# Attention values in a vision-transformer kernel: two half-array products per head pair instead of one full-array product

## The reference, cut to what matters

```python
q = (x @ Wq).reshape(b, n, H, DH)      # b = 64 images, n = 17 tokens, H = 16 heads, DH = 64
k = (x @ Wk).reshape(b, n, H, DH)
v = (x @ Wv).reshape(b, n, H, DH)
scores = einsum('bihd,bjhd->bhij', q, k) * scale + bias      # ALiBi slope per head
scores = where(causal, scores, -1e30)
attn = softmax(scores)
out = einsum('bhij,bjhd->bihd', attn, v).reshape(b, n, H * DH)
return out @ Wo + bo
```

## Time and profile before

| what | value |
|---|---|
| median of three runs | 633.22 us (632.42 to 634.51) |
| span of the profiled execution | 671.0 us |
| PE busy / weight loads busy | 545.3 / 438.7 us |
| DVE / ACT / POOL busy | 439.3 / 358.8 / 218.8 us |
| mean granted TensorE clock of the profiled execution | 0.908 |
| line 942 (values), PE passes and busy time | 256, 32.1 us |
| line 1381 (its copies), ACT instructions and busy time | 128, 35.6 us |

### The profile page before, as it was taken

One profiled execution on the slowest core, in us unless ns is written; L12 is line 12 of the kernel. 1 busy time (PEld: TensorE's weight loads), 2 busy tenths in 40 slices (PEclk: granted clock), 3 DMA queues, 4 the chain that ended last, 5 costly groups with the idle time before them and its releaser, 6 DMA issues.

```text
span 671.0 us, 9955 instructions
## 1 busy us (share of the span) xinstructions
PE 545.3 (81%) x3242; PEld 438.7 (65%) x3242; DVE 439.3 (65%) x995; ACT 358.8 (53%) x894; POOL 218.8 (33%) x230
## 2 busy tenths in 40 slices
PE   3969760565546999999999999999889789888976
PEld 3737650133236899999998878776556557566675
DVE  4987998999994455555555137575646646654576
ACT  1667624355546677777773464255545645565610
POOL 2010001134226011111112312566656666666400
PEclk9977985668857999999999999999979989998878
DMA  8960000054000000000000020056646657565583
GB/s 279 382 235 0 1 0 0 0 194 133 2 0 1 24 25 25 24 25 25 1 1 1 1 68 9 18 169 180 183 135 197 169 147 212 163 204 166 144 363 104
DMA packets 43894, 67.31 MB, mean 100 GB/s; under 512 B 11022, under 2 KB 27015, under 8 KB 43716
## 3 DMA queue, kind: packets, MB, share of 16 engines
q1 hardware_dynamic: 36868, 64.62, 30.3%
q0 software_dynamic: 6976, 2.07, 1.5%
HBM read 66.81 MB, written 17.20 MB: 125 GB/s over the span
## 4 chain that ended last, share of the span: by engine, by line
PE 56%; DVE 26%; ACT 6%; issue 5%; another core or an unknown queue 3%; DMA 1%; POOL 1%; SPq 0%; ACTq 0%; DVEq 0%
PE ps L1089 9%; PE ps L736 6%; PE ps L734 6%; PE ps L735 6%; PE ps L953 5%; PE ps L911 4%; PE ps L942 4%; PE ps L741 3%; PE ps L1097 2%; PE ps L925 2%; PE ps L1079 2%; DVE region L1731 2%; PE ps L1136 2%; DVE region L1742 1%
## 5 line engine op out<-in xcount | busy, mean ns | idle before, releaser
L1089 PE MATMUL ps<-region 128*128 128x352 f32 x256 | 93.0, 488 | 5.9 <-issue 3.1
L694 POOL DMA_INDIRECT y_rows<-region x60 | 62.2, 1037 | 58.1 <-ACT region L1433 39.1
L1787 DVE TENSOR_TENSOR region<-ps,region 32x136 f32<-32x136 f32 x128 | 38.1, 297 | 60.1 <-PE ps L911 58.6
L685 POOL DMA_INDIRECT region<-x_rows,region x64 | 68.1, 1064 | 20.2 <-issue 17.4
L734 PE MATMUL ps<-nTh,high 128*128 128x272 f32 (+2 forms) x248 | 74.1, 299 | 0.4 <-ACT region L1362 0.4
L735 PE MATMUL ps<-nTl,high 128*128 128x272 f32 (+2 forms) x248 | 71.7, 289 | 0.0
L644 POOL COPY region<-region 32x544 f32<-32x544 f32 x32 | 26.4, 825 | 122.2 <-DVE region L1806 120.7
L1456 ACT ACTIVATE high<-region 88x512 fp32r<-88x512 f32 x64 | 40.3, 630 | 43.2 <-remote 23.1
L1089 PEld LDWEIGHTS ps<-region 128*128 128x128 f32 x256 | 45.7, 199 | 24.5 <-issue 7.3
L1935 DVE SCALAR_TENSOR_TENSOR region<-region,ps 128x176 f32<-128x176 f32 x64 | 25.3, 396 | 53.3 <-ACT region L1446 24.4
L736 PE MATMUL ps<-nTh,pairs_low 128*128 128x272 f32 x192 | 55.4, 289 | 0.0
(11 more groups left out here) (264 smaller groups left out, 1439.3 us busy)
## 6 DMA issues: line engine op xcount, KB each, us to landing
region<-moe_w SPq DMA_DIRECT2D x64, 352.0 KB
region<-moe_w SPq DMA_DIRECT2D x64, 176.0 KB
y_rows<-zrow SPq DMA_DIRECT2D x1, 6528.0 KB, 25.3
region<-y_rows SPq DMA_DIRECT2D x8, 768.0 KB, 10.7
region<-wqkv SPq DMA_DIRECT2D x8, 384.0 KB, 3.0
region<-ffn_w SPq DMA_DIRECT2D x2, 1024.0 KB, 8.3
region<-patches SPq DMA_DIRECT2D x3, 384.0 KB, 8.3
region<-patches SPq DMA_DIRECT2D x1, 1152.0 KB, 10.7
```

Source lines behind the costliest of these rows:

```text
L685: nc.gpsimd.indirect_dma_start(out=xb[m8], out_offset=None, in_=x_rows, in_offset=bass.IndirectOffsetOnAxis(ap=sloti[:, at:at + 1], axis=0 ...
L694: nc.gpsimd.indirect_dma_start(out=y_rows, out_offset=bass.IndirectOffsetOnAxis(ap=sld[m8], axis=0), in_=yb[m], in_offset=None, bounds_che ...
L1089: mm = nc.tensor.matmul(ps[:, 2 + m % 2, 0:2 * EI], xbT[m % 2][:, c, :], w13[m][:, c, :], start=(c == 0), stop=(c == DC - 1))
L1787: last = V.tensor_tensor(sc[r, s0:s0 + 8, 0:T].rearrange("p (a b) t -> p a b t", a=4), ps[r, 4:8, 0:4 * GW].rearrange("p a (b h t) -> p a ...
```

## The change

The values block has four PSUM banks of eight products in place of eight banks of two. Each product takes one head: 64 stationary columns, 68 moving columns, and a result on partitions 0 to 63 (head 0) or 64 to 127 (head 1) of the same bank and the same columns. The two heads alternate. All 4 x 68 = 272 columns of a bank are then useful, in the order of `attnT`, so ACT empties a bank with one copy of 128 x 272. The fills of a pair go from 24 to 20 (HPF = 5), which moves the semaphore counts, and `scores(1)` comes after the second of four banks instead of the fourth of eight.

```diff
-HPF = 6
+HPF = 5
@@ def attention(n, j):   (and the same count in move and before project)
-                first = 0 if isinstance(n, int) and n == 0 else 4 * HPF * n - 8
+                first = 0 if isinstance(n, int) and n == 0 else 4 * HPF * n - 4
...
                     if n == HP:
-                        pe.wait_ge(s_evac, 4 * HPF * n - 8)
-                    both = pbd[1 - j].rearrange("p (h g) w -> p g h w", h=2)
-                    for g in range(8):
-                        if project and g == 4:
+                        pe.wait_ge(s_evac, 4 * HPF * n - 4)
+                    for g in range(4):
+                        if project and g == 2:
                             scores(1)
                         b = fill(g if not project else 16 + g)
-                        for k in range(2):
-                            mm = nc.tensor.matmul(ps[:, b, 2 * k * GW:2 * (k + 1) * GW].rearrange("p (h w) -> p h w", h=2),
-                                                  vp[1 - j][:, 2 * g + k, :], both[:, 2 * g + k, :, :],
-                                                  start=True, stop=True)
+                        for k in range(4):
+                            for hd in range(2):
+                                f = slice(DH * hd, DH * hd + DH)
+                                mm = nc.tensor.matmul(ps[f, b, k * GW:(k + 1) * GW], vp[1 - j][:, 4 * g + k, f],
+                                                      pbd[1 - j][:, GT * hd + 4 * g + k, :], start=True, stop=True)
                         mm.then_inc(s_fill, 1)
@@ def move(n, j):
                 if not (isinstance(n, int) and n == 0):
-                    for g in range(8):
+                    for g in range(4):
                         act.wait_ge(s_fill, first + 1 + g)
-                        for hd in range(2):
-                            f = slice(DH * hd, DH * hd + DH)
-                            cs = slice(2 * g * GW, 2 * (g + 1) * GW)
-                            dst = attnT[f, n - 1, cs] if isinstance(n, int) else \
-                                attnT[f, bass.ds(n - 1, 1), cs].rearrange("p a b -> p (a b)")
-                            ins = nc.scalar.activation(
-                                dst.rearrange("p (k w) -> p k w", k=2),
-                                ps[f, g % 4, 0:4 * GW].rearrange("p (k h w) -> p k h w", k=2, h=2)[:, :, hd, :], ACT.Copy)
-                        ins.then_inc(s_evac, 1)
+                        nc.scalar.activation(attnT[:, n - 1, 4 * g * GW:4 * (g + 1) * GW], ps[:, g, 0:4 * GW],
+                                             ACT.Copy).then_inc(s_evac, 1)
```

More of the change, by code:

```diff
@@ L959, in _ @@
             pe.wait_ge(s_ext, 2 * HP)
-            pe.wait_ge(s_evac, 4 * HPF * HP - 8)
+            pe.wait_ge(s_evac, 4 * HPF * HP - 4)
             for t in range(4):
```

## The result

The changed kernel takes 622.91 us (median of four runs, 620.44 to 625.0) against 633.78 us (632.42 to 634.51) of the kernel before, run beside it: a ratio of 0.984 with a 95% interval of 0.980 to 0.987, 10.9 us less. The profiled execution of the changed kernel has a span of 623.3 us, near its own runs; that of the kernel before had 671.0.

What follows compares the result with a forecast made beforehand. PE was taken to bound blocks 1 to 7; seven blocks -9.5, last values -2.6 and the stall before the output projection -0.5 gave -12.6 us, 633.2 to 620.6 us; range 618.5 to 636.5 us.

Steps and rivals of the forecast that it cites:

- The overlap: Values of a block: both heads' passes run side by side on array halves, 31 ns each, 1.98 us against 3.71; chance 0.53.
- the turns: Values: the array halves take turns, passes one after another at 59 ns, 633.4 to 636.5 us; chance 0.37.
- The first rival: Values: the halves take turns at 59 ns a pass, +1.9 us, 635.1 us, up to 636.5 with 62 ns; chance 0.37.
- The second and third rivals: Values: each change of half drains, 658 us; or one half's loads stop the other's products, 663 us; together chance 0.07.
- The changes of shape: Switches between full-array and narrow products in a block: four at 0.094 us each, 0.38 us added.
- Copies: ACT's value copies: sixteen become four, 3.1 us less on ACT per block, worth nothing in blocks 1 to 7.
- Last values: Values of n = 8, first pass to line 953: 5.43 us becomes 2.81, -2.6 us.
- The stall before the output projection: Last pass of pair 6's values to line 953: 1.41 us becomes 0.87 as ACT finishes sooner, -0.5 us.
- Waits that come closer: In a block, scores(1) stays hidden behind DVE by 0.2 us; key copies counted as nothing, at worst 0.2 us a block.

Runs made afterwards that it cites:

- e9: Changed kernel with head 1's products sent to head 0's partitions, so all passes use one array half; 1.006 of the kernel before, block period 18.92 us.
- e3: Changed kernel with a block's values in one piece behind both halves of the scores, two shape changes fewer; 0.983 of the kernel before, period 16.96 us.
- e1: Changed kernel with head 0's four products of a bank first, then head 1's four, instead of alternating; 0.994 of the kernel before, block period 17.84 us.
- e8: Changed kernel with the heads alternating after every two products instead of every one; 0.984 of the kernel before, block period 17.16 us.
- e2: Changed kernel with ACT emptying each bank by four copies of 64 x 136 instead of one; 0.988 of the kernel before, block period 17.04 us.
- e5: e3 with ACT's rounding of the next weights moved behind the key copies; 651.5 us, 0.980 of the kernel before, block period 16.71 us.
- e6: Changed kernel with scores(1) in two parts, six shape changes a block instead of four; 0.990 of the kernel before, periods 17.60 and 17.66 us.
- e4: Kernel before, with its full-array products and two copies a bank, in the order of e3; 1.005 of the kernel before, block period 18.52 us.
- e7: Changed kernel with each head's 64 value columns as two products of 32, on array quarters; 0.987 of the kernel before, block period 17.01 us.
- the second group: Kernels run on another chip beside the kernel before; the unchanged changed kernel, rerun there, took 656.3 us against 665.1, ratio 0.987.

## Why the prediction was right

**The overlap** was the step on which all hung, and it held: 32 passes in 0.945 us from first to last start, 29.5 ns each, against 31 forecast. It was inferred from the delays at changes of shape, which is a thin reason, so the choice between it and the turns was partly luck; the range, 618.5 to 636.5 us, holds both. e9 is what shows the overlap, with the same passes at twice the time on one half.

**The first rival** was priced at 635.1 us, up to 636.5. e9 is that case built, at 0.6% over before (0.3 to 0.8), some 637 us on the scale of the first chip. Its kind and sign were right; it was short by the changes of shape. One reason given for it, that PE starts products in order, is what the starts of e1 and e8 speak against. The second and third rivals would have put 0.15 and 0.11 us between starts; the steady ones are 6 or 7 and 53 ns.

**The changes of shape** are the term that was mis-sized: 0.094 us forecast, 0.38 a block. What the rows of before gave me was only the later start of the next product. The second pass after a change is late as well. In the changed kernel the way in costs 0.093 at the start and 0.05 at the second couple, 0.14 in all; the way out 0.094 and 0.10, 0.20. A second pass 0.22 us behind the first also follows a plain wait (e3, 267.32 to 267.54), so this part is not peculiar to changes of shape. Four changes cost 0.68 us a block. With this, 32 x 0.116 = 3.71 before, 64 x 0.0296 = 1.89 and 0.68 after, gives -1.14, and the period fell by 1.13. The forecast was -1.35. The page "TensorEngine Tiling (Array Packing)" of the Trainium skill, section "Tiling Modes", says that a change of tiling mode drains TensorE; the late first and second passes agree with that, and put these prices on it.

**Copies** in blocks 1 to 7: worth nothing, as forecast (e2). **Last values:** 2.61 us against 2.81 forecast, -2.8 instead of -2.6.

**The stall before the output projection** was wrong in sign. The forecast took off 0.5 us because ACT would be done sooner. The time from the last pass of values to line 953 rose from 1.41 to 1.74 us (347.62 + 0.94 = 348.56 to 350.30): when ACT is early, DVE is late. `project` writes banks 4 to 7 and has to wait until DVE has read `scores(1)`; DVE ended at 350.20 now, and before the change it had ended at 356.61, only 0.3 us ahead of ACT at 356.95. The shorter the values behind `scores(1)`, the less of this read they hide. DVE in order of time, kernel before; then DVE and ACT, changed kernel:

```profile
354.14 2.47 DVE L1787 TENSOR_TENSOR region<-ps,region 32x136 f32<-32x136 f32 x8 [2.98 <-PE ps L911]
```

```profile
347.73 2.47 DVE L1780 TENSOR_TENSOR region<-ps,region 32x136 f32<-32x136 f32 x8 [2.42 <-PE ps L911]
348.36 0.87 ACT L1376 ACTIVATE region<-ps 128x272 f32<-128x272 f32 x2 [2.28 <-PE ps L943]
```

ACT was done at 348.36 + 0.87 = 349.23, 0.67 us behind the start of the last pass of values; with the 0.14 to PE that is 0.81, so the forecast's 0.87 was right for ACT, and wrong in taking ACT for the last. Where DVE and ACT end within 0.04 us of each other (e5, e9), the same time is 0.81 and 0.80 us.

The misses, 0.2 us a block and 0.8 us at the stall, less 0.1 us on the last values and the change of shape ahead of them, are the distance between -12.6 forecast and -10.5 found in the trace.

**Waits that come closer:** the forecast left `scores(1)` a margin of 0.2 us and the key copies almost none. Neither became a wait in the changed kernel. Both became one when an experiment took a little more: the first in e6, the second in e3 and e4.

## What to carry to other kernels

If a product fills half of the array's columns with a result that nobody reads, split it into products on separate column ranges and let them alternate: here the column count stayed and the products took half the time (3.71 to 1.89 us a block). Put all such products in one piece, since each change between half-array and full-array products cost 0.14 to 0.20 us here, and check the second pass after the change, not the first alone. Then look at what the new order waits for: in e3 it took back three quarters of the gain of 0.34 us a block. When a bound stretch gets shorter, list every semaphore that its end waits for, with the time at which each is met: the second latest takes over.

## What the runs showed of the hardware

- Narrow fp32 products of 68 columns: 59 ns a pass on one half (e9), two side by side on halves, four on quarters (e7), starts 6 to 7 ns apart. The loads run side by side too: they start in the same couples (259.271 and 259.277).
- PE seems not to keep strict program order between halves: with eight passes of one half in a row, what looks like the other half's first pass starts beside the fifth (e1); with four in a row, 13 ns after the first (e8). The Trainium skill, "TensorE: Matmul & The Clock Gate", section "Part 3: Packing small matmuls — row/col tiling", says that products start and end in program order; the starts of e1 and e8 speak against it, as far as records that don't name the half can. They speak as well against the sentence ahead of the prediction that the order in the source is the order on the engine, for passes on different halves.
- The same program differs between chips in the expert stage. In the two traces below, both of the changed kernel, it takes 197.0 us at 216 GB/s and 233.4 us at 182 GB/s, with the attention's period at 17.04 us in both.

Busy time by stretch, the experts to the end, changed kernel on the first chip and on that of the second group:

```profile
426.22:623.22 197.00, 183.47 (x1048) 141.91 (x1048) 138.38 (x402) 112.83 (x319) 124.22 (x120) 0.98 0.71 216
```

```profile
422.83:656.23 233.40, 200.54 (x1048) 147.08 (x1048) 139.48 (x402) 112.80 (x319) 125.30 (x120) 0.93 0.61 182
```

The profiled execution of the kernel before had 235.2 us there, which is why its span was 671.0 us and its runs 633; what differs between the chips was not looked into.
